# Fp32 projections for the first row of an attention and mixture-of-experts kernel, with its weight loads and splits reordered

## The reference

```python
q, k, v = x @ wq, x @ wk, x @ wv                  # 16 heads, 4 key heads, 128 each
q, k = rms_norm(q, q_norm_w), rms_norm(k, k_norm_w)
k_ctx, v_ctx = rms_norm(h_ctx_kv @ wk_ctx, k_norm_w), h_ctx_kv @ wv_ctx
q = q * cos + rotate_half(q) * sin                # and k
probs = softmax(q @ [k_ctx, k].T * scale + mask)
out = (probs @ [v_ctx, v]) @ wo
...
x = x + _L0_xattn_ref(_layernorm(x, axis=-1), ctx_2048, ...)
x = x + _L0_ffn_ref(_layernorm(x, axis=-1), ...)  # top 2 of 8 experts, and a shared one
```

## Time and profile before

| | us |
|---|---|
| median of 3 executions | 361.87 |
| lowest, highest | 360.94, 363.26 |
| the profiled execution, its own time | 360.24 |
| its span, first to last instruction | 357.6 |

### The profile page before, as it was taken

How to read it: one execution, slowest core, us unless ns; L and a number is a source line. 1 busy time by engine, 2 the same in 40 slices (tenths; PEclk the granted TensorE clock), 3 DMA queues, 4 the chain that set the end, 5 groups by cost and what they waited for, 6 DMA issues and landing times.

```text
span 357.6 us, 7425 instructions
## 1 busy us (share of the span) xinstructions
PE 326.2 (91%) x2292; PEld 222.8 (62%) x2296; DVE 313.5 (88%) x602; ACT 263.6 (74%) x917; POOL 166.4 (47%) x241
## 2 busy tenths in 40 slices
PE   6677698799999999999999999999999999999994
PEld 5354465377657765766576667666766687856452
DVE  1779999998999899989998999899989997875763
...
GB/s 185 385 242 235 18 0 2 1 2 15 1 61 115 15 0 68 107 15 3 59 0 15 0 0 0 15 0 0 0 0 0 1 2 0 2 88 90 135 165 114
DMA packets 34834, 19.24 MB, mean 54 GB/s; under 512 B 24056, under 2 KB 32256, under 8 KB 34816
## 3 DMA queue, kind: packets, MB, share of 16 engines
...
...
## 4 chain that ended last, share of the span: by engine, by line
PE 37%; DVE 22%; ACT 19%; issue 11%; POOL 6%; DMA 2%; SPq 1%; DVEq 1%; ACTq 0%; POOLq 0%
PE proj L1362 10%; ACT probs L548 8%; PE pt_ps L1325 6%; DVE probs L982 6%; PE turn L1271 4%; POOL q_rot L774 3%; PE o_ps L1335 3%; DVE nmax L970 3%; DVE pT_lo L908 3%; PE proj L1182 3%; ACT pT_hi L459 3%; PE sc_ps L1292 3%; ACT kc_junk L492 2%; DVE q_t L899 2%; DMA wq<-in_L_xattn_wq_dram 2%
## 5 line engine op out<-in xcount | busy, mean ns | idle before, releaser
L548 ACT ACTIVATE probs<-sc_ps,nbias,q_r 128x256 f32<-128x256 f32 x128 | 70.8, 573 | 2.8 <-DVE nbias L974 2.8
L774 POOL TENSOR_TENSOR q_rot<-q_t 128x512 f32<-128x512 f32 x32 | 42.4, 1325 | 41.3 <-DVE q_t L901 40.5
L982 DVE TENSOR_SCALAR probs<-probs,rden 128x256 f32<-128x256 f32 x128 | 51.0, 459 | 1.1
L459 ACT ACTIVATE pT_hi<-pt_ps 128x512 f16<-128x512 f32 x64 | 34.8, 597 | 10.2 <-PE pt_ps L1325 10.2
L492 ACT ACTIVATE q_junk<-proj 128x128 bf16<-128x128 f32 x128 | 34.1, 298 | 10.8 <-DVE q_t L901 10.8
L908 DVE SCALAR_TENSOR_TENSOR pT_lo<-pt_ps,pT_hi 128x512 f16<-128x512 f32 x64 | 41.0, 681 | 0.1
L1182 PE MATMUL proj<-wq_hi,xT 128*128 128x512 f16 x128 | 38.2, 380 | 2.7 <-DVE wq_lo L892 2.2
L970 DVE TENSOR_REDUCE nmax<-sc_ps 128x4 f32<-128x1024 f32 x32 | 38.8, 1214 | 1.5 <-PE sc_ps L1314 1.5
L459 ACT ACTIVATE qT_hi<-turn 128x512 f16<-128x512 f32 x32 | 19.5, 609 | 21.6 <-PE turn L1271 21.6
L731 POOL TENSOR_TENSOR q_r<-q_me,power 128x4 f32<-128x4 f32 x32 | 33.4, 1044 | 2.5
L1325 PE MATMUL pt_ps<-ident,probs 128*128 128x128 f32 x256 | 34.2, 278 | 0.2
...
## 6 DMA issues: line engine op xcount, KB each, us to landing
wq<-in_L_xattn_wq_dram SPq DMA_DIRECT2D x4, 512.0 KB, 7.9
...
wq<-in_L_xattn_wo_dram SPq DMA_DIRECT2D x1, 2048.0 KB, 8.2
...
wkc<-in_L_xattn_wk_ctx_dram SPq DMA_DIRECT2D x1, 512.0 KB, 4.0
wk<-in_L_xattn_wk_dram SPq DMA_DIRECT2D x1, 512.0 KB, 5.0
```

What stands on the lines that cost most here:

```text
L459: return nc.scalar.activation(out_, in_, ACT.Copy, scale=scale)
L548: last = nc.scalar.activation(probs[:, h, :], sc_ps[:, h, :], ACT.Exp, bias=nbias[:, h:h + 1], scale=q_r[:, g, h:h + 1], accum_out=den[:, ...
L774: nc.gpsimd.tensor_tensor(q_rot[:], q_t1[:], q_t2[:], ALU.add).then_inc(q_added, 1)
L982: last = nc.vector.tensor_scalar(probs[:, h, :], probs[:, h, :], rden[:, h:h + 1], None, ALU.mult)
```

## The change

For row 0 the layer-normed input is turned and kept in fp32 (`xT32`, in the memory of `xT`), and the projections of q, k and v multiply it in fp32 with the unsplit weights (`project_exact`, two matmuls where there were six). So row 0 needs no split of `wk`, `wq` or `wv`; the splits are needed from row 1 on and are spread over row 0. `x_hi` and `x_lo` of row 0 fall away. The tables and norm weights are loaded from ACT's queue. SP loads in the order `x`, `wk`, `ctx`, `wkc`, `wq[0]`, and then waits for a landing before each next batch. The load of `wo` waits also for all four fp32 projections of q. The keys of row 0 are turned into the two banks of `pt_ps`. The first `q_rot` is added by DVE and no more by POOL. `keep_warm` calls fall from 116 matmuls to 56.

```diff
@@ key_banks, row 0's keys in pt_ps @@
+            if isinstance(nb, int) and nb == 0:
+                return pt_ps[:, 1, :], pt_ps[:, 0, :]
+            return turn[:], proj[0][:]
@@ SP @@
             sp.dma_start(x_all[:, 0:1, :], xt[:, 0:1, :]).then_inc(d_x0, 16)
+            sp.dma_start(wk32[:], parts(wk)).then_inc(d_wk, 16)
             sp.dma_start(ctx_b[:], ctx[0, :, :]).then_inc(d_ctx, 16)
             sp.dma_start(wkc[:], parts(wk_ctx)).then_inc(d_wkc, 16)
...
+            load_wq(0)
+            sp.wait_ge(d_wk, 16)
+            load_wq(1)
+            sp.wait_ge(d_wkc, 16)
+            sp.dma_start(wvc[:], parts(wv_ctx)).then_inc(d_wvc, 16)
+            sp.dma_start(wv32[:], parts(wv)).then_inc(d_wv, 16)
+            sp.wait_ge(d_wq[0], 16)
+            load_wq(2)
+            load_wq(3)
...
+            sp.wait_ge(q_proj, G)
             sp.wait_ge(w_lo, G + 1)
             sp.dma_start(wo32, parts(wo)).then_inc(d_wo, 16)
@@ ACT @@
+            nc.scalar.dma_start(kw_sb[:], k_norm_w.partition_broadcast(P)).then_inc(d_tab, 16)
+            nc.scalar.dma_start(cos_sb[:], cos).then_inc(d_tab, 16)
...
+                    copy(flat(xT32), turn[:, 0:256], W_SCALE).then_inc(xT_ready, 1)
...
+                    if isinstance(nb, int) and nb == 1:
+                        act.wait_ge(q_proj, G)
+                        act.wait_ge(v_proj, 1)
...
+            split_wq(0)
+            k_squares(0)
             kc_squares(0)
...
+            split_wq(1)
             q_squares(0, 1)
-            act.wait_ge(d_wv, 16)
-            split_high(wv32[:], wv_hi[:])
-            wc_split(1)
+            split_wq(2)
@@ ACT, row @@
+                    if first and g == 0:
+                        split_wq(3)
+                        wc_split(0)
+                    if first and g == 2:
+                        act.wait_ge(d_wv, 16)
+                        split_high(wv32[:], wv_hi[:])
+                        wc_split(1)
                     if first and g == 1:
                         wo_split(0)
                         wo_split(1)
@@ DVE @@
+            k_turn(0)
+            k_add(0)
+            split_low(wk32[:], wk_hi[:], wk_lo[:], 1)
             q_turn(0, 0)
+            dve.wait_ge(q_t12, 1)
+            nc.vector.tensor_tensor(q_rot[:], q_t1[:], q_t2[:], ALU.add).then_inc(q_added, 1)
+            split_wq(0)
...
@@ DVE, row, ahead of q_low @@
                     if first and g == 0:
-                        split_low(wv32[:], wv_hi[:], wv_lo[:], G + 2)
+                        split_wq(2)
+                    if first and g == 1:
+                        wc_split(0)
@@ DVE, row, behind normalise @@
-                    if g == 1 and first:
+                    if g == 0 and first:
+                        split_wq(3)
+                    if g == 2 and first:
+                        split_low(wv32[:], wv_hi[:], wv_lo[:], G + 2)
+                    if g == 3 and first:
                         wc_split(1)
@@ PE @@
+            def project_exact(bank, w, cols, signal):
+                for c in range(DC):
+                    last = nc.tensor.matmul(bank[:], xT32[:, c, :], w[:, c, cols], start=(c == 0), stop=(c == DC - 1))
+                last.then_inc(signal, 1)
```

More of the change, by code:

```diff
@@ L1014, in _, with split_wq @@
             ln_scale(0)
-            split_low(wk32[:], wk_hi[:], wk_lo[:], 1)
-            split_low(wq32[:, :, 0:GW], wq_hi[:, :, 0:GW], wq_lo[:, :, 0:GW], 2)
-            wc_split(0)
+            def split_wq(g):
+                cols = slice(g * GW, (g + 1) * GW)
+                split_low(wq32[:, :, cols], wq_hi[:, :, cols], wq_lo[:, :, cols], g + 2)
             dve.wait_ge(c_tab, 2)
@@ L1435, in row @@
                         turn_probs(b, g)
-                    if first and g < 2:
-                        pe.wait_ge(w_lo, g + 4)
+                    if first and g >= 2:
+                        pe.wait_ge(w_lo, g)
                     if ahead_of(b, g, 2, last):
```

135 lines of the change are left out of this document (67 added, 68 removed).

## The result

| | before | after |
|---|---|---|
| median of 6 executions each, us | 362.55 | 371.69 |
| lowest, highest | 360.74, 363.68 | 370.29, 372.31 |
| the profiled execution, its own time | 360.24 | 372.31 |
| its span | 357.6 | 370.6 |

The ratio is 1.0273, with a 95% interval of 1.0241 to 1.0304: the changed kernel is slower, by 9.1 us of the medians. The two profiled executions lie 12.1 us apart, since the one of before lies 2.3 us under its median and the one of after 0.6 over, and their spans 13.0. One of the four executions of a later run (the pass in four) took 1901.69 us and is left out of its ratio.

A forecast was written before the change was run, and what follows sets the result against it. Row 0 was taken as bound by DVE, later rows by PE. Terms -4.5 + 3.5 + 0 + 1.9 + 3.5 + 1.2 + 1.0 = +6.6 us on the median of 361.87 gave 368.5 us, range 361 to 374.

The forecast's parts named there:

- the clock rival: Rival, chance 0.15: waits in steps 0 and 2 drop PE to its lower clock more often, +3.3, 371.8 us.
- The start: Stretch up to row 0's first maximum: `k_t` 5.3 us earlier, at 9.6, less 0.8 for a longer chain: -4.5 us.
- The rival of shared loads: Rival, chance 0.08: tables on ACT's queue slow `wk` and `ctx`, the start gains only 3.0 us, total 370.0 us.
- Step 0: First of row 0's four steps: DVE waits 1.9 us for a high half, pass 1.2, projection 0.5: +3.5 us.
- Step 1: Second step of row 0: the low half of `wvc` is only exchanged for that of `wkc`: 0.
- Step 2: Third step of row 0: two costs through ACT's order, +1.9 and +3.5 us, predicted +5.4 in the ledger.
- The first of its two costs: Step 2: `wo`'s load is issued later, ACT gets through later, DVE's `qT_lo` starts at 49.2: +1.9 us.
- The second: Step 2: `wv_hi` stands behind ACT's key squares; DVE waits from 53.86 to 56.1, its pass takes 1.2: +3.5 us.
- Step 3: Fourth step of row 0: DVE's low half of `wvc` is added, +1.2 us.
- Contention: Start of row 1: POOL's and DVE's two-input SBUF passes hold one another up; middle of 0.1 and 1.9 taken, +1.0 us.
- Waits covered: Rival, chance 0.17: high halves and `wo` come in time, so 1.9 and 2.3 go from step 2: +2.4, 364.3 us.
- Faster: Rival, chance 0.10: row 0's low halves cost nothing, PE sets its end, only the start counts: -4.5, 357.4 us.

The follow-up runs named there:

- the pass in four: Changed kernel with POOL's single `wo_lo` pass cut into four instructions of a quarter each: 1.0145 of the kernel before.
- the version with all four edits: Changed kernel with tables staged after `x`, fourth `wq_lo` pass ending step 0, `wv` passes ahead of `wo`'s, POOL's `wo_lo` in four: 358.53 us, 0.9934.
- the run that it is held against: Kernel before, with only POOL's `wo_lo` pass cut into four pieces: 0.9942 of the kernel before.
- the two edits of step 2: Changed kernel with ACT's `wv` and `wvc` passes moved to step 1 (1.0121), then also its first two `wo` passes to step 2 (1.0161).
- The version with matmuls in its waits: The version with all four edits, plus 34 and 46 unread matmuls in PE's waits in steps 1 and 3: 358.50 us, 0.9905.

## Why the prediction was right, and where its steps failed

The direction and its reason were right: DVE binds row 0, so what is put there is paid in full, and the start gives less than the row takes. 371.69 us lies in the range of 361 to 374, 3.2 us above the 368.5, and all but on the clock rival's 371.8. That closeness is luck: the rival has no late start in it, and the sum of +6.6 stands against 12.1 us between the two profiled executions (13.0 between their spans), so the sum was mis-sized more than the medians show.

**The start** is the step that failed most: -4.5 predicted, -1.9 measured. By the forecast's own sign, a first `nmax` after 24.4, it was wrong there (25.45). The working of the chain held: from `k_t` to the first `nmax` it said 13.3 us and 13.1 were measured. What failed is "`k_t` at 9.6" with all loads taken as in time. It was 12.37. The rival of shared loads named the cause but looked at `wk` and `ctx`; it was `x`, at the head of the first queue, which the tables held up by 2.6 us. At full pace `k_t` came at 11.23, so of the missing 2.8 us 1.1 are PE's half pace and the other 1.6 go with the late `x`: in the version with all four edits, with `x` in time and PE at full pace, the key projection was done at 9.70. There the first `nmax` comes at 23.43, a gain of 3.95 on the ledger's 27.38 (4.5 on the 27.93 of the run that it is held against), and `k_t` at 10.51, where it waits for the tables.

**Step 0**: +3.5 against +3.3, with DVE's wait for `wq_hi` of 1.9 against 1.83. Right by its own steps, though their sum, 1.9 + 1.2 + 0.5, is 3.6. **Step 1**: 0 and 0.

**Step 2**: +5.4 against +6.8. The first of its two costs was right: counted from the start of step 1, `qT_lo` stood at 47.32 - 35.90 = 11.4 before, was forecast at 49.2 - 35.9 = 13.3 and came at 50.68 - 37.25 = 13.4, with `wo`'s load issued 2.6 us into the step (2.5 forecast) and 8.3 us on the way (8.2). The second was the term mis-sized: DVE's wait for `wv_hi` was 3.64 us for 2.3, because PE made the keys at the lower clock and ACT's squares of them, ahead of `wv_hi`, came later. With the clock kept up the wait is 2.35 us, as forecast, and the step 1.4 us shorter, which is that difference.

**Step 3**: +1.2 against +1.4. **Contention**: +1.0 taken between 0.1 and 1.9; `nbias` took 1.26 more. The direction was right, but not the picture, since not DVE's pass but `nbias` was held up longer: DVE's `wvc` pass (72.55) was over before POOL began, and the added time is `nbias` alone, which came earlier within POOL's pass.

**The clock** was a rival at 0.15 and should have been a term. The ledger's 12.8 exceed the sum of 6.6 by 6.2 us. Of these 1.4 are the low clock in step 2 and 2.0 that in step 0 of row 1; with them the rival's price of +3.3 was about right. The start has 2.6 more, of which 1.2 is PE's half pace and the rest goes with the late `x`. The remainder is the contention (+0.3), step 3 (+0.2) and step 0 (-0.2). The clock doesn't replace the forecast's mechanism: it comes on top of waits that the forecast adds.

**Waits covered** was wrong as a forecast of this kernel, and the two edits of step 2 made it true: the waits go by reordering. **Faster** was wrong, and stayed so: in the version with all four edits row 0 still gives back 4.2 us, so the low halves aren't free there.

What stays open is why the clock falls after one wait and not after another of equal length: after PE's 2.54 us in step 0 it stayed up in the changed kernel and fell in the two kernels with the tables behind `x`. It is also open whether PE's half pace at the start, with a recorded clock of 1.00, is the low clock. The Trainium skill says (TensorE: Matmul & The Clock Gate, Part 1: The HAM clock gate) that the same kernel shows different numbers of slow matmuls at its start from run to run. The traces agree in durations: with the same instructions up to there, the key projection took 1.98 us in one run and 2.49 to 3.61 in five. The version with matmuls in its waits fits it as well: 361.18 us and a mean clock of 0.987 in the execution with a spell in step 0, 358.3 to 359.1 us and 0.992 to 0.999 in the other six, of which no trace was kept.
